# The last stage in one block with the two before it, its first batch amid the end of the rotary attention

## The reference

```python
q, k = apply_rope(x @ Wq + bq), apply_rope(x @ Wk + bk)      # 16 heads of 8
attn = softmax(q k^T / sqrt(8)); out = (attn v) @ Wo + bo
x = layernorm(x + out)                                        # r3 in the kernel

weights = x @ w_r + b_r                                       # [4, 1024]
threshold = top_k(weights, 512)[-1]
hidden = gelu(x @ W1 + b1)                                    # [4, 1024, 512]
blk = hidden @ W2 + b2
x = layernorm(x + where(weights > threshold, blk, x))
```

## Time and profile before

| | us |
|---|---|
| median of the three runs | 1937.72 |
| lowest, highest | 1935.43, 1938.97 |
| the profiled execution | 1932.66 |
| its span, first to last instruction | 1930.9 |
| PE busy in it | 1739.3 (90%) |
| DVE busy | 1136.8 (59%) |
| ACT busy | 1274.8 (66%) |
| POOL busy | 939.5 (49%) |

### The profile page before, as it was taken

One profiled execution on the slowest core, in us unless ns is written; L12 is line 12 of the kernel. 1 busy time (PEld: TensorE's weight loads), 2 busy tenths in 40 slices (PEclk: granted clock), 3 DMA queues, 4 the chain that ended last, 5 costly groups with the idle time before them and its releaser, 6 DMA issues. The chain is left out here.

```text
span 1930.9 us, 25433 instructions
## 1 busy us (share of the span) xinstructions
PE 1739.3 (90%) x8942; PEld 832.9 (43%) x8942; DVE 1136.8 (59%) x1868; ACT 1274.8 (66%) x2447; POOL 939.5 (49%) x566
## 2 busy tenths in 40 slices
PE   7888479999999999999999999879999999998695
PEld 3443345545554445554454555324333333332264
DVE  5888597986668876588766566531423223120286
ACT  2121215766767677767577666768998999999543
POOL 3556206778876778757798678860000000000033
PEclk9999689999999999999999999989999999999898
DMA  2000100000000000000000000130221312201001
GB/s 72 1 1 0 35 11 11 21 21 11 21 11 22 11 21 11 22 11 21 11 22 20 12 11 11 33 131 23 66 88 31 123 40 70 74 36 36 1 12 35
DMA packets 27863, 59.04 MB, mean 31 GB/s; under 512 B 3840, under 2 KB 14800, under 8 KB 27728
## 3 DMA queue, kind: packets, MB, share of 16 engines
q1 hardware_dynamic: 27728, 57.32, 9.2%
HBM read 38.44 MB, written 18.87 MB: 30 GB/s over the span
## 5 line engine op out<-in xcount | busy, mean ns | idle before, releaser
L742 POOL TENSOR_TENSOR b_psum<-b_psum,b_probs 128x1024 f32<-128x1024 f32 x192 | 461.5, 2404 | 181.1 <-ACT b_probs L886 174.9
L2193 ACT ACTIVATE c_probs<-banks 128x1024 f32<-128x1024 f32 x512 | 483.5, 1029 | 46.0 <-PE banks L2242 35.1
L1268 DVE TENSOR_TENSOR b_gated<-banks,b_g 128x480 f32<-128x480 f32 x512 | 314.2, 655 | 229.4 <-PE banks L987 224.5
L886 ACT ACTIVATE b_probs<-banks 128x1024 f32<-128x1024 f32 x256 | 254.0, 1018 | 226.5 <-PE banks L1020 225.7
L987 PE MATMUL banks<-b_w,b_xh 128*128 128x480 f32 x1024 | 353.9, 400 | 32.7 <-DVE b_gated L1268 18.6
L1276 DVE TENSOR_REDUCE b_tok<-b_gated 128x192 f32<-128x960 f32 x256 | 281.3, 1138 | 0.5
L1020 PE MATMUL banks<-b_qq,b_kk 64*128 64x512 f32 x1024 | 262.2, 623 | 10.2 <-DVE b_gated L1268 10.0
L857 ACT ACTIVATE b_share<-b_o,b_picked 128x64 f32<-128x64 f32 x1080 | 268.7, 337 | 1.5 <-DVE b_o L1301 1.5
L1052 PE MATMUL banks<-b_probs,b_tok 128*64 128x512 f32 x1024 | 252.2, 614 | 2.2 <-ACT b_probs L886 2.2
L2257 PE MATMUL banks<-c_probs,c_vg 128*32 128x512 f32 x2048 | 249.4, 605 | 2.9 <-DVEq L2300 2.6
L987 PEld LDWEIGHTS banks<-b_w,b_xh 128*128 128x128 f32 x1024 | 195.2, 191 | 115.6 <-issue 40.0
(11 more groups left out here) (243 smaller groups left out, 1877.0 us busy)
## 6 DMA issues: line engine op xcount, KB each, us to landing
b_raw_w<-in_L_ffn_W SPq DMA_DIRECT2D x32, 480.0 KB, 3.4
c_heads<-c_split SPq DMA_DIRECT2D x24, 512.0 KB
c_keys<-c_heads SPq DMA_DIRECT2D x16, 512.0 KB, 3.6
c_queries<-c_heads SPq DMA_DIRECT2D x16, 512.0 KB, 4.6
c_heads<-c_split SPq DMA_DIRECT2D x8, 384.0 KB
a_xs<-in_L_attn_x SPq DMA_DIRECT2D x4, 512.0 KB, 8.0
out<-d_yo SPq DMA_DIRECT2D x3, 512.0 KB, 3.6
c_heads<-c_split SPq DMA_DIRECT2D x8, 128.0 KB
```

What stands on the lines that cost most here:

```text
L742: nc.gpsimd.tensor_tensor(psum[:, par, :], prev, probs[:, i % 4, :], ALU.add).then_inc(psum_rdy, 1)
L886: nc.scalar.activation(probs[:, i % 4, :], score_b[i % 2], ACT.Exp).then_inc(exp_rdy, 1)
L1268: nc.vector.tensor_tensor(shape(gated[:, t % 2, j, :]), shape(proj_b[u % WAYS][:, 0:HALF_W]), g.unsqueeze(2).broadcast_to([P, 3, HD2, E]), ...
L2193: nc.scalar.activation(probs[:, step % 4, c, :, :], unit_b[u % NU], ACT.Exp, scale=float(HD) ** -0.5).then_inc(exp_rdy, 1)
```

## The change

`depth_lead` is no longer a block of its own: its instructions for each engine follow the rotary stage's in the block of the two stages before. Its tiles start at the same place in SBUF as before, but leave out the first bytes (`spared`), where weights of the rotary stage lie that its ending still reads. On PE and DVE the rotary body now ends after its last products (PE) or the last pair's division (DVE) and returns the rest as a generator, `left`, which the last stage's body advances at chosen points:

- PE: `turn_x(0)`, the turn of pair 7, `router_row(0)`, `turn_out` 0, `router_column(0)`, `expand(0,0)`, `project_out` 0, `expand(0,1)`, `turn_out` 1, `project_out` 1, the sum of the counts (now in bank 6), a wait for all DVE reads of them; then `turn_x(1)`, `router_row(1)` and on as before.
- DVE: the four pieces with the count's steps between them, the flag, `choose(0)`, the norm of batch 3, then `choose(1)` and on as before.

ACT, POOL and SP run the last stage's list straight behind the rotary stage's. The clearing of the middle semaphores moves from POOL's start of the last stage into `redo_all`, with a drain and a signal `cleared`, for which each engine waits inside the redo branch only.

```diff
 # rotary_led, tensor
             for back in (2, 1):
                 products(B - 1, BS - back)
-            turn(B - 1, NP - 1, z_index(B, 0) - NX)
-            turn_counts(nc, pe, judged, good, ident, unit_b[0][0:1, 0, 0:P])
-            for k, (kind, half) in enumerate(Z_PIECES):
-                piece(z_index(B, k) - NX, kind, half, B - 1, B * NP)
+            def left():
+                turn(B - 1, NP - 1, z_index(B, 0) - NX)
+                yield
+                for k, (kind, half) in enumerate(Z_PIECES):
+                    piece(z_index(B, k) - NX, kind, half, B - 1, B * NP)
+                    yield
+                turn_counts(nc, pe, judged, good, ident, acc_b[0:1, 0:P])
+                pe.wait_ge(used, z_index(B, NZ) - NX)
+                pe.wait_ge(judged, 5)
+            return left()
 # rotary_led, vector
             normalize(B - 1, NP - 1)
-            count_safe(nc, dve, judged, recips[:, :], ok[:, :], good)
-            for k, (kind, half) in enumerate(Z_PIECES):
-                piece(z_index(B, k) - NX, kind, half, B - 1)
-                if k == 1:
-                    raise_flag(...)
-            norm(B - 1)
+            def left():
+                counted = safe_parts(nc, dve, judged, recips[:, :], ok[:, :], good)
+                for k, (kind, half) in enumerate(Z_PIECES):
+                    next(counted, None)
+                    piece(z_index(B, k) - NX, kind, half, B - 1)
+                raise_flag(...)
+                yield
+                norm(B - 1)
+            return left()
 # depth_lead
+        if kept_from is not None:
+            sb("spared", [P, spared // 4])
 ...
         @block.tensor
-        def _(pe):
+        def _(pe, left=iter(())):
             turn_x(0)
+            next(left, None)
             router_row(0)
+            next(left, None)
             router_column(0)
             for b in range(B):
                 expand(b, 0)
+                if b == 0:
+                    next(left, None)
+                    expand(0, 1)
+                    for _ in left:
+                        pass
                 if b + 1 < B:
                     turn_x(b + 1)
-                expand(b, 1)
+                if b:
+                    expand(b, 1)
 ...
         @block.vector
-        def _(dve):
+        def _(dve, left=iter(())):
+            next(left, None)
             choose(0)
+            for _ in left:
+                pass
 # redo_all, gpsimd
-            past.clear(pool)
+            for past in pasts:
+                past.clear(pool)
+            pool.drain().then_inc(cleared, 1)
             with only_if(pool, flag):
+                pool.wait_ge(cleared, 1)
 # program, in the block of the two stages before
-                    rotary.tensor_body(pe)
+                    ending.tensor_body(pe, rotary.tensor_body(pe))
-                    rotary.vector_body(dve)
+                    ending.vector_body(dve, rotary.vector_body(dve))
-            depth_lead(nc, r3, out_dram, ps, ident, I, nc.Block(), depth, middle, weights, lead.kept_from, "d_")
```

More of the change, by code:

```diff
@@ L1925, in __init__ @@
         self.b_all = sb("b_all", [P, 2, D])
+        self.spared = self.end - self.base
         self.cos, self.sin = sb("cos", [P, T]), sb("sin", [P, T])
@@ L2382, in _ @@
             normalize(B - 1, NP - 1)
-            count_safe(nc, dve, judged, recips[:, :], ok[:, :], good)
-            for k, (kind, half) in enumerate(Z_PIECES):
-                piece(z_index(B, k) - NX, kind, half, B - 1)
-                if k == 1:
-                    raise_flag(nc, dve, judged, unit_b[0][0:1, 0, 0:P], total, P * (lead.COUNTS + B * H * NT), flag[0:1, 2:3])
-            norm(B - 1)
+            def left():
[3 more added lines that the diff above has]
+                    piece(z_index(B, k) - NX, kind, half, B - 1)
+                raise_flag(nc, dve, judged, acc_b[0:1, 0:P], total, P * (lead.COUNTS + B * H * NT), flag[0:1, 2:3])
+                yield
+                norm(B - 1)
+            return left()
     return out
@@ L2410, in load, with depth_lead @@
         sp.dma_start(self.w2[:, :, :], I["L1_ffn_W2"].rearrange("(n p) c -> p n c", p=P)).then_inc(self.w2_in, 16)
-def depth_lead(nc, x, out_dram, ps, ident, I, place, signals, past, weights, kept_from, tag):
+def depth_lead(nc, x, out_dram, ps, ident, I, place, signals, past, weights, kept_from, spared, tag):
     FF = 512
@@ L2708, in _, with redo_all @@
             last_norm(B - 1)
-def redo_all(nc, r1, r2, out_dram, ps, ident, I, past, flag):
+def redo_all(nc, r1, r2, out_dram, ps, ident, I, pasts, flag):
     signals = Signals(nc)
     sem = signals.names("redo_")
-    met = sem("met")
+    met, cleared = sem("met"), sem("cleared")
+    for past in pasts:
+        past.release()
     expert, rotary, depth = Programs(), Programs(), Programs()
@@ L2726, in redo_all @@
         weights = DepthWeights(lambda name, shape: held.enter_context(nc.sbuf_tensor("d_redo_" + name, shape, F32)), sem)
-        depth_lead(nc, r3, out_dram, ps, ident, I, nullcontext(depth), signals, None, weights, None, "d_redo_")
+        depth_lead(nc, r3, out_dram, ps, ident, I, nullcontext(depth), signals, None, weights, None, 0, "d_redo_")
         def meet(eng, count):
@@ L2738, in _ @@
             with only_if(sp, flag):
+                sp.wait_ge(cleared, 1)
                 expert.sync_body(sp)
@@ L2759, in _ @@
             with only_if(act, flag):
+                act.wait_ge(cleared, 1)
                 expert.scalar_body(act)
@@ L2769, in _ @@
             with only_if(pe, flag):
+                pe.wait_ge(cleared, 1)
                 expert.tensor_body(pe)
@@ L2779, in _ @@
             with only_if(dve, flag):
+                dve.wait_ge(cleared, 1)
                 expert.vector_body(dve)
@@ L2806, in program @@
             recips = held.enter_context(nc.sbuf_tensor("recips", [P, RotaryLead.COUNTS + B * H * NT], F32))
-            expert, rotary = Programs(), Programs()
+            expert, rotary, ending = Programs(), Programs(), Programs()
             lead = RotaryLead(nc, middle, r2, ps, ident, I, "c_")
@@ L2811, in program @@
             weights = DepthWeights(lambda name, shape: lead.place("d_" + name, shape), depth.names("d_"))
+            linear.release()
+            depth_lead(nc, r3, out_dram, ps, ident, I, nullcontext(ending), depth, None, weights, lead.kept_from, lead.spared, "d_")
             with nc.Block() as block:
@@ L2816, in _ @@
                     rotary.sync_body(sp)
+                    ending.sync_body(sp)
                 @block.gpsimd
@@ L2821, in _ @@
                     rotary.gpsimd_body(pool)
+                    ending.gpsimd_body(pool)
                 @block.scalar
@@ L2826, in _ @@
                     rotary.scalar_body(act)
+                    ending.scalar_body(act)
                 @block.tensor
@@ L2835, in _ @@
                     expert.vector_body(dve)
-                    rotary.vector_body(dve)
-            linear.release()
-            depth_lead(nc, r3, out_dram, ps, ident, I, nc.Block(), depth, middle, weights, lead.kept_from, "d_")
-            middle.release()
-        redo_all(nc, r1, r2, out_dram, ps, ident, I, depth, flag)
-        depth.release()
+                    ending.vector_body(dve, rotary.vector_body(dve))
+        redo_all(nc, r1, r2, out_dram, ps, ident, I, (middle, depth), flag)
 def constants():
```

3 lines of the change are left out of this document (2 added, 1 removed).

## The result

| | before | changed |
|---|---|---|
| median of five runs, us | 1937.72 | 1927.48 |
| lowest to highest | 1935.43 to 1940.68 | 1922.97 to 1928.35 |
| profiled execution, its span | 1932.66, 1930.9 | 1922.97, 1921.0 |
| ratio | | 0.9946 (0.9931 to 0.9962) |

The changed kernel is faster by 0.54%, 10.2 us in the medians and 9.9 us in the spans.

What follows compares the result with a forecast made beforehand. It took PE to bound the last stage before, and DVE's queue with the change; `bn_aggr` 8.9 us earlier minus 0.2 for the moved clear gives 8.7, so 1937.72 becomes 1929.0 us, range 1924 to 1933.5.

Steps and rivals of the forecast that it cites:

- The seam: From the last products to the first choice: `choose(0)` starts at 1827.4 instead of 1843.0, 15.6 us earlier.
- The norm beside `keep(0)`: Norm of batch 3 on DVE behind `choose(0)`, stretched by POOL's `keep(0)`: 10.5 us instead of 6.8.
- rival B: Norm of batch 3 not stretched, or only partly: gain 12.7, 1925.0 us (PE alone the bound: 16.4, 1921.5); chance 0.14.
- DVE's chain: DVE's queue from `choose(0)` on has no gap from 1827.4; batch 3's `bn_aggr` follows at 1906.15, the later chain.
- PE's chain: PE's contractions in the last stage: contraction 3 ends at 1903.5 (before 1912.97), its gather and statistics at 1905.6.
- rival C: PE's clock falls: at `turn_x(2)` 1.7 against 2.3 slack, costing nothing; earlier, before `choose(0)`, gain 6, 1931.5 us; chance 0.12.
- a clock of 0.5 in the contractions: Sign in the last stage: a granted PE clock of 0.5 during contractions would show the forecast wrong.
- The end: After `bn_aggr`: same norm and output instructions; semaphore clear moved to the redo block costs 0.2 us, ends 0 and 0.5.
- The sum: Whole kernel: `bn_aggr` 8.9 us earlier, minus 0.2, gives 8.7 us gained, 1929.0 us.

Runs made afterwards that it cites:

- the norm behind the first gather: Changed kernel with DVE's norm of batch 3 moved from behind `choose(0)` to behind batch 0's gather, statistics and guess; ratio to before 0.9938, interval 87.85 us.
- tighter pieces: Against "the norm behind the first gather": on PE `project_out` 0 ahead of `expand(0,0)`, second-half pieces and count sum ahead of `expand(0,1)`; ratio to before 0.9934, interval 87.83 us.
- plain concatenation: Changed kernel's single block with nothing interleaved, whole rotary ending and norm first; ratio to before 0.9931, interval 87.15 us; repeat 0.9915, 90.68 us.

## Why the prediction was right, point by point

**The seam.** `choose(0)` was put 12.5 us after the last products and came at 12.8. The hand-overs, the order of the pieces and the hidden table load are as counted, each step up to 0.3 us later.

**The norm beside `keep(0)`.** Predicted 10.5, measured 10.2. The instructions blocked weren't quite those that the sum named. L75 and L76 did get through before POOL's third operation. By the rows alone the Newton steps were then free, and without L79's 2.0 us the norm would have taken 8.2 (the prediction says about 8.6). They weren't free, as L79's 2.20 us shows: the rule of the Trainium skill ("SBUF — State Buffer", "Who interferes with whom") that a DVE operation with two SBUF inputs waits for a reading GpSimd operation is borne out, and it is what kept the term at its size. The sum's own terms had both TENSOR_SCALARs, or the second of them, wait for the third operation; the number held because a TENSOR_TENSOR waited in their place. The experiment with `keep(0)` held back gave 3.4 for the term, as against 3.7 in the sum. It also made rival B's condition true, and its time was nearly B's: 12.45 us off the interval, where B said 12.7.

**DVE's chain.** Choices at 33.4, 50.2 and 66.9; predicted 33.3, 50.2 and 67.1. DVE had no idle time from the first choice to the guess of batch 2, 70.9 us, as forecast. The chain of waits goes through DVE, and "the norm behind the first gather" confirms that its members, not their places, count.

**PE's chain.** Contraction 1 began 45.0 after the last products (predicted 44.9); contractions 2 and 3 ended at 73.1 and 88.6 (predicted 73.1 and 88.6). Contraction 0 began at 21.2 instead of 20.4, with no effect. The clock fell once in each of the two traces of the changed kernel. In the second it fell in the wait before `turn_x(2)`, where rival C put it. There it took 2.8 us of PE's time, not the 1.7 of the text, against 2.2 of slack, not 2.3, and contraction 1 began 0.65 later; the interval stayed within 0.1 us, so "costs nothing" was right with some luck in the sizes. In the first trace that wait (3.37 us) was followed by no fall, and the clock fell in contraction 1 instead, behind a wait of 2.8 (9.01 us instead of 7.41, granted clock 0.56 from 1859.5 to 1863.0). That is one of the signs that the prediction itself named as wrong, a clock of 0.5 in the contractions. It cost nothing either, for a reason that the text had counted but not tied to it: PE's `router_row(3)` waited for ACT, which had batch 0's outputs to give out first.

What the clock costs where it isn't covered is shown on the neighbours: 2.4 us with the norm ahead of the first choice, 3.2 of PE's time with tighter pieces, 3.5 in the repeat of plain concatenation.

**The end.** 0.2 us were put down for clear, drain and signal in the redo block; from `bn_aggr` to the end of the span it took 15.83 against 15.85 before. The term is zero.

**The sum.** Interval 8.9 predicted, 9.08 measured. The median fell by 10.2 instead of 8.7. In the profiled executions 0.8 of the rest is ahead of the seam. For the medians this can only be argued: in thirteen traces with the same code there, the last products ended anywhere from 1813.1 to 1824.6, so a median of five runs can carry some us of that, and part of the closeness of 1927.48 to 1929.0 is luck. A slip of 0.2 in rival B changes nothing: 16.4 below 1937.7 is 1921.3, not 1921.5.

**What the prediction didn't see.** The sum was right for the change as a whole, but treated it as one thing. It isn't: where PE's clock held, the removed block and the count's new place give 13.0 us, and the interleaved order takes 3.9 back, 3.4 of it by the norm that POOL stretches. The text priced the norm's stretch and never asked what the interval would be without the interleaving.

## What to carry to other kernels

When a phase of one engine is moved out of another's way, it still stands in a queue: add up that queue to the end of the kernel, and look at what runs on POOL beside it. A reordering that removes waits can be judged only with PE's clock: look for the waits which it opens elsewhere, read the granted clock behind each, and profile more than once, as one trace can show a fall that the next doesn't. And take a change apart before calling it good: here its simplest part had the shorter interval in both traces, by 3.9 and 0.5 us, and one added wait on POOL was worth 3.4.

## What the runs showed of the hardware that I had not expected

A DVE TENSOR_TENSOR of 8 columns lasted 2.20 us instead of 0.17 while POOL ran a 128x1024 operation, and a TENSOR_SCALAR of 8 columns 1.55 to 1.74. Both show as long instructions, not as idle time, so no list of waits names them. Beside the same POOL operations bn_stats (1.64 us for eight), `bn_aggr`, the comparisons with accumulation (1.27 us each, with or without POOL) and the gathers, which read one operand from PSUM, kept their times.

PE's clock isn't a function of the program: the same list of instructions ran its pieces at 1.00 once and at 0.50 another time, 87.15 against 90.68 us for the interval. In the changed kernel the same wait of 3.4 us was followed by no fall in one trace and by a fall in the other. Nor did a fall need a long wait: it came behind 2.8 us in the first trace of the changed kernel, 1.8 with the norm behind the first gather (contraction 2 took 9.01 us there too), and amid pieces with no wait above 0.88.
